# The last attention layer: output projection spread over the recurrence, key sum as a 129th column

## The chip, the cores and the metric

The kernel runs on one core of a Trainium2 chip. The metric is the device time of one execution in microseconds. The program is a chain of four transformer-like layers, each with an attention half and a feed-forward half; the change is inside one half, the attention of the last layer (layer 3).

## The reference

The stream x is one sequence of T = 1024 tokens with D = 256 features. In layer 3 there are H = 16 heads of 128, and the tokens are taken in segments of 64. For each head a memory matrix `mem` (128 x 128) and a divisor `z` (128) are carried from segment to segment:

```python
def step(carry, seg):
    mem, z = carry
    qq, kk, vv = seg
    sigma_q = jax.nn.elu(qq) + 1.0
    scores = jnp.einsum('bhsk,bhtk->bhst', qq, kk) / scale
    scores = jnp.where(causal_mask, scores, -jnp.inf)
    att_dot = jax.nn.softmax(scores, axis=-1) @ vv
    att_mem = sigma_q @ mem / (sigma_q @ z)
    sigma_k = jax.nn.elu(kk) + 1.0
    delta = vv - sigma_k @ mem / (sigma_k @ z)
    mem_new = mem + jnp.einsum('bhsk,bhsv->bhkv', sigma_k, delta)
    z_new = z + sigma_k.sum(axis=-2, keepdims=True).transpose(0, 1, 3, 2)
    att = beta * att_mem + (1.0 - beta) * att_dot
    out = att.reshape(Bsz, SEG, H * DV) @ Wo
    return ((mem_new, z_new), out)
# mem starts at 0, z at 1/128; q, k, v = h @ Wq, h @ Wk, h @ Wv, and x = x + gate * out
```

`att.reshape` lays the heads end to end: rows 4h to 4h + 3 of a segment come from head h alone, and the j-th block of 128 in row 4h + r is that head's token 16r + j of the segment. So the output projection needs, for each j of 0 to 15, four tokens (r = 0 to 3) of every segment of a head, and a pair of heads fills 2 x 64 rows.

## The kernel before

Everything is float32. Features lie on partitions and tokens along the free axis. `l3_attention` (L1917) works through the 16 heads in 8 pairs (numbered 0 to 7 here; `a` is the head in the pair, 0 or 1). Each engine has its own queue, written out by hand as a function `pair(i, ...)`: TensorE from L2024, ScalarE from L2191, VectorE from L2298. The engines meet through semaphores alone, so a wait holds up everything behind it in its queue. PSUM has eight banks of 512 columns. SyncE loads the next pair's weights once the current pair's projections are done, and GpSimd only prepares constants.

The start of a pair on TensorE, in this order: `projections(0)` (keys and queries of head 0, banks 4 to 7, 24 matmuls of 512 columns, L2036), `project_out(i)` (the output projection of the pair before, 32 matmuls, L2021), `scores(0)` (L2068), `values()` for both heads (L2044), `keys_by_token(0)` (turns the keys, L2055), `projections(1)`, `keys_by_token(1)`, `scores(1)`. ScalarE beside it: `queries_keys` (exp into `e`, L2197, and a copy into `qk`, L2198) for each 512 columns; `place_keys`, `values_copy`, `exponential` of the scores (L2226) and `keys_copy` (even half of the partitions, L2210). VectorE: `sigma` (elu + 1 in two instructions, L2307 and L2314), `key_sums` (L2320, L2325), the softmax (`read_scores` L2345, `largest` L2351, `shift` L2354, `total` L2359 and L2360, `normalize` L2364), the odd halves of `values_copy` (L2334) and `keys_copy` (L2340), and `add_projection` (L2296), which adds the projected result of the pair before to x.

Then comes the recurrence, 15 steps n = 1 to 15 for both heads. A step is `read_memory(n, a)` for both heads on TensorE (L2091: keys and queries of the segment times `mem`; column 128 of `mem` holds the divisor), then a filler, then `write_memory(n, a)` (L2080), which adds the keys times the delta to the memory that stays in banks 4 and 5. Between them lies a round through two engines: VectorE's `delta` (L2370 reciprocal of the divisor, L2373) makes `dr` from the read, and ScalarE's `mem_copy` (L2221) carries the memory from PSUM to `mem` after the write.

`key_sums(a)` makes all 16 divisors of a head ahead of the recurrence: one sum over each segment's keys, then a running sum in four additions.

The fillers now: `turn_probs` (turns the softmax, L2101) at steps 1, 2, 7 and 8; `local_attention` (L2114), in halves, at steps 3 to 6 and 9 to 12; `turn_reads` (L2127, turns what the queries read) at 13 and 14, and the rest of it after step 15. ScalarE copies or scales what a filler made (`probs_copy` L2230, `dot_scale` L2235) and prepares the next pair's weights (`high_part` L2189); VectorE does the second head's softmax, `low_part` and, at the end, `add_reads` (L2380), which mixes both parts into `att`.

A segment's 64 tokens are ordered by j, then by r (the permutation `turn` does that). `att` lives in the buffer of the layer's normalised input in the projection's order: for each j the 4 tokens of all 16 segments of a head lie in one run of 64. So `local_attention` and `turn_reads` put each segment's 64 columns into PSUM as 16 pieces of 4 columns (16 bytes) through `segment_rows`, and `project_out` reads two runs of 64 elements.

## Time and profile before

| | us |
|---|---|
| median of 3 runs | 2037.61 |
| lowest, highest | 2035.45, 2040.75 |
| the profiled execution | 2039.76 |
| its span, first to last instruction | 2038.0 |
| mean granted clock of TensorE, as a share | 0.933 |
| l3_attention's eight pairs, from 1352.8 to about 1908 | 555 |
| starts of the pairs in the span | 1352.8, 1419.1, 1488.3, 1558.4, 1627.7, 1696.9, 1766.9, 1837.1 |

The profile is of one execution. A timeline row gives start, length, engine, line, what is written from what, the shape and a count; in square brackets stand the idle time of the engine before it and who ended it. A float32 matmul shows as two records; a matmul with the hi and lo parts shows as one. Records of matmuls overlap, so a record's length is its latency, and the rate is the distance from start to start. A group row gives busy us and the mean in ns, then the idle time before the group's instructions and who ended it.

### The profile page before, as it was taken

The numbers are of one execution on the slowest core, as the hardware profiler recorded it, in microseconds if no ns is written. First come the engines' busy times: TensorE is split into PE (matmuls) and PEld (weight loads), VectorE is DVE, ScalarE is ACT, GpSimd is POOL, SyncE is SP. The second block draws the span as 40 slices with busy tenths as digits, with TensorE's granted clock in tenths as the row PEclk, the third lists the DMA queues.
The fourth block names the chain that finished last, engine by engine and source line by source line (L and its number), as shares of the span: only waits on it lengthen the run. The fifth ranks groups of instructions, "written<-read, shape, count | busy, mean of one in ns | idle before, by whom it ended". The sixth has DMA issues, their size and how long they took to land. (4 is left out here: it accounts for less than half of the span.)

```text
span 2038.0 us, 27403 instructions
## 1 busy us (share of the span) xinstructions
PE 1781.8 (87%) x9315; PEld 1440.3 (71%) x9315; DVE 1081.2 (53%) x2163; ACT 872.8 (43%) x1690; POOL 243.9 (12%) x236
## 2 busy tenths in 40 slices
PE   5988786987689999999787969969999899999898
PEld 4676645775568888888644858857888788878755
DVE  2266435233545555555656345566665676567466
ACT  3466424333243343333675334354443444344344
POOL 2010002212022222222101212220000000000000
PEclk8999886998789999999898979979999999999989
DMA  2000030110034334332100023210000000000100
GB/s 103 6 14 11 0 132 0 39 31 0 18 101 114 108 110 118 115 108 82 52 0 15 32 57 114 82 58 17 17 16 0 15 15 15 0 15 0 41 0 21
DMA packets 47075, 91.50 MB, mean 45 GB/s; under 512 B 7697, under 2 KB 24081, under 8 KB 46810
## 3 DMA queue, kind: packets, MB, share of 16 engines
q1 hardware_dynamic: 47026, 90.89, 14.9%
q8 instruction: 26, 0.43, 0.1%
q14 instruction: 23, 0.19, 0.0%
HBM read 89.52 MB, written 1.35 MB: 45 GB/s over the span
## 5 line engine op out<-in xcount | busy, mean ns | idle before, releaser
L438 PE MATMUL bank<-l1m_src_hi,l1m_w_hi 128*128 128x512 f32 x384 | 150.2, 391 | 7.4 <-DVE l1m_src_lo L507 7.4
L438 PE MATMUL bank<-l1m_src_lo,l1m_w_hi 128*128 128x512 f32 x384 | 150.0, 391 | 0.0
L438 PE MATMUL bank<-l1m_src_hi,l1m_w_lo 128*128 128x512 f32 x384 | 149.9, 390 | 0.0
L410 POOL TENSOR_TENSOR l1m_w_lo<-l1m_w,l1m_w_hi 128x512 fp32r<-128x512 f32 x96 | 104.8, 1110 | 325.9 <-ACT l1m_w_hi L475 325.9
L514 DVE TENSOR_TENSOR l1m_a<-l1m_s,bank 128x512 f32<-128x512 f32 x96 | 66.0, 687 | 116.3 <-ACT l1m_s L487 116.3
L491 ACT ACTIVATE l1m_a_hi<-l1m_a 128x512 fp32r<-128x512 f32 x96 | 60.7, 633 | 146.5 <-DVE l1m_a L520 146.5
L2091 PE MATMUL bank<-l_mem,l_sg 128*128 128x129 f32 x480 | 95.0, 316 | 30.2 <-ACT l_mem L2221 15.4
L2091 PEld LDWEIGHTS bank<-l_mem,l_sg 128*128 128x128 f32 x480 | 67.9, 195 | 55.8 <-ACT l_mem L2221 44.4
L528 DVE TENSOR_TENSOR l1m_a_lo<-l1m_a,l1m_a_hi 128x512 fp32r<-128x512 f32 x96 | 66.4, 692 | 70.8 <-ACT l1m_a_hi L491 70.8
L2370 DVE RECIPROCAL l_inv<-bank 128x1 f32<-128x1 f32 x240 | 38.9, 162 | 115.4 <-PE bank L2091 115.4
L2221 ACT ACTIVATE l_mem<-bank 128x128 f32<-128x128 f32 x240 | 59.8, 276 | 90.5 <-PE bank L2080 90.0
L2080 PE MATMUL bank<-l_dr,l_nkt 128*128 128x128 f32 x480 | 89.8, 304 | 8.3 <-ACT l_dr L2249 8.0
L487 ACT ACTIVATE l1m_s<-bank 128x512 f32<-128x512 f32 x96 | 57.4, 598 | 87.7 <-PE bank L438 87.7
L438 PEld LDWEIGHTS bank<-l1m_src_hi,l1m_w_hi 128*128 128x128 f32 x384 | 72.5, 189 | 24.1 <-issue 9.1
L2373 DVE SCALAR_TENSOR_TENSOR l_dr<-bank,l_inv,l_v 128x128 f32<-128x128 f32 x240 | 84.2, 351 | 8.5
L438 PEld LDWEIGHTS bank<-l1m_src_lo,l1m_w_hi 128*128 128x128 f32 x384 | 72.5, 189 | 15.1
L438 PEld LDWEIGHTS bank<-l1m_src_hi,l1m_w_lo 128*128 128x128 f32 x384 | 72.5, 189 | 15.0
L2080 PEld LDWEIGHTS bank<-l_dr,l_nkt 128*128 128x128 f32 x480 | 68.4, 196 | 17.1 <-ACT l_dr L2249 7.9
L452 PE MATMUL bank<-l1m_a_hi,l1m_w_hi 128*128 128x512 f32 x192 | 74.8, 390 | 0.8 <-DVE l1m_a_lo L528 0.8
L452 PE MATMUL bank<-l1m_a_lo,l1m_w_hi 128*128 128x512 f32 x192 | 74.7, 389 | 0.0
L452 PE MATMUL bank<-l1m_a_hi,l1m_w_lo 128*128 128x512 f32 x192 | 74.7, 389 | 0.0
L2501 POOL MEMSET l3f_imp<- 96x2048 f32 x1 | 1.8, 1806 | 573.7 <-POOLq L88 573.7
(537 smaller groups left out, 4561.9 us busy)
## 6 DMA issues: line engine op xcount, KB each, us to landing
l1m_w<-in_l1f_win SPq DMA_DIRECT2D x48, 256.0 KB, 2.9
l1m_wr<-l1f_token_weights SPq DMA_DIRECT2D x32, 384.0 KB, 3.5
l1m_wr<-l1f_token_weights SPq DMA_DIRECT2D x32, 256.0 KB, 3.9
l_w<-in_l_w SPq DMA_DIRECT2D x9, 768.0 KB, 4.4
wmod<-in_wmod SPq DMA_DIRECT2D x4, 1536.0 KB, 10.1
l1m_w<-in_l1f_wout SPq DMA_DIRECT2D x48, 128.0 KB, 3.1
l1m_wr<-l1f_token_weights SPq DMA_DIRECT2D x32, 128.0 KB, 3.2
l2e_wr<-l2f_token_weights SPq DMA_DIRECT2D x16, 256.0 KB, 3.9
```

Source lines behind the costliest of these rows:

```text
L410: pool.tensor_tensor(w_lo[:, half, part], w[:, half, part], w_hi[:, half, part].bitcast(F32), ALU.subtract).then_inc(split_, 1)
L438: last = pe.matmul(k.bank[:, 2 * c + part, :], wq[:, half, at:at + P], xq[:, b, chunk(c)], start=(b == 0 and q == 0), stop=(b == DB - 1 an ...
L452: last = pe.matmul(k.bank[:, 4 + 2 * m + c, :], wq[:, half, at:at + P], aq[:, c, :], start=(first and q == 0 and not extra), stop=False, s ...
L487: act.activation(s[:, c, :], k.bank[:, 2 * c, :], ACT.Silu).then_inc(act_ready, 1)
L491: act.activation(a_hi[:, c, :], a[:, c, :], ACT.Identity).then_inc(hi_ready, 1)
L514: last = dve.tensor_tensor(a[:, c, :], s[:, c, :], k.bank[:, 2 * c + 1, :], ALU.mult)
L528: dve.tensor_tensor(a_lo[:, c, :], a[:, c, :], a_hi[:, c, :].bitcast(F32), ALU.subtract).then_inc(lo_ready, 1)
L2080: pe.matmul(k.bank[:, MEM + a, 0:P], nkt[:, a, n // 2, n % 2, :], dr[:, a, n, :], start=(n == 0), stop=False, skip_group_check=True).then_ ...
L2091: pe.matmul(k.bank[:, READ + a, 0:P + 1], sg[:, a, n // 2, at:at + 2, :], mem[:, a, n, 0:P + 1], start=True, stop=True).then_inc(s["read_r ...
L2221: act.activation(mem[:, a, n + 1, 0:P], k.bank[:, MEM + a, 0:P], ACT.Identity).then_inc(s["mem_copied"], 1)
L2370: dve.reciprocal(inv[:, a, n % 2:n % 2 + 1], k.bank[:, READ + a, P:P + 1]).then_inc(s["inv_ready"], 1)
L2373: dve.scalar_tensor_tensor(dr[:, a, n, :], k.bank[:, READ + a, 0:P], inv[:, a, n % 2:n % 2 + 1], v[:, n // 2, a, n % 2, :], ALU.mult, ALU. ...
```

## The change

- `project_out` leaves the start of a pair. It is cut in 7 parts (`Y_AT`) of 5, 5, 5, 5, 4, 4 and 4 matmuls, the fillers of steps 1 to 7; `add_projection` moves to step 8. The result bank is 3 instead of 4, and `local_attention(0, 1)` waits for `x_added`.
- The other fillers move back: `turn_probs` for both halves at steps 8 and 10, `local_attention`, now whole, at 9, 11, 12 and 13, `turn_reads` at 14 and 15. ScalarE's `probs_copy`, `dot_scale` and `high_part` and VectorE's `low_part` move with them. All four `add_reads` come after step 15.
- `key_sums` is gone, and the wait for `z_ready` with it. `dr` has a 129th column of -1, and `write_memory` multiplies the negated keys by 129 columns, so the key sum builds up in column 128 of the bank; `first_divisor` puts 1/128 there, and `mem_copy` copies 129 columns. `mem` has 2 slots instead of 16.
- `att` keeps each segment's 64 columns together. `local_attention` and `turn_reads` write 64 columns in one run, and `project_out` reads, for each j, 32 pieces of 4 elements (16 bytes) through `att_by_row`.
- In the start `values()` goes ahead of `scores(0)` and waits for `reads_added`. ScalarE does both `values_copy` ahead of `exponential(0)`, both halves of `keys_copy(0)`, and `place_keys(1)` last. VectorE does both `values_copy` ahead of `read_scores(0)`, and `sigma(4)` and `sigma(5)` ahead of `total(0)`. The banks of values and scores are exchanged.

```diff
+    MEM, READ, Y, SCORES = 4, 6, 3, (5, 0)
+    V_BANKS = (0, 2)
+    Y_AT = (0, 5, 10, 15, 20, 24, 28, 32)
...
+        first_z = sb("first_z", [P, P + 2])
+        mem = sb("mem", [P, HP, 2, P + 2])
+        dr = sb("dr", [P, HP, NS, P + 2])
...
-            return rows_of(bank)[:, :, n * R:(n + 1) * R]
+        att = k.h
+        att_by_row = k.h[:].rearrange("p a (g j r) -> p (a g) j r", j=H, r=R)
...
-                step.link(pool, pool.memset(z[:], 0.0))
-                step.link(pool, pool.memset(z[:, 0, :, PAD:PAD + 1], 1.0 / P))
+                step.link(pool, pool.memset(first_z[:], 0.0))
+                step.link(pool, pool.memset(first_z[:, P:W1], 1.0 / (P * P)))
+                step.link(pool, pool.memset(dr[:, :, :, P:P + 2], -1.0))
...
-                def project_out(turn):
-
-                    pe.wait_ge(s["att_ready"], turn * HP)
-                    for m in range(DB):
-                        for j in range(H):
-                            last = pe.matmul(k.bank[:, Y, m * P:(m + 1) * P], wo[:, j, tile(m)], att[:, :, j, :],
-                                             start=(j == 0), stop=(j == H - 1))
-                    last.then_inc(s["y_ready"], 1)
+                def project_out(turn, part):
+
+                    if part == 0:
+                        pe.wait_ge(s["reads_added"], turn * 4)
+                    for mj in range(Y_AT[part], Y_AT[part + 1]):
+                        m, j = mj // H, mj % H
+                        last = pe.matmul(k.bank[:, Y, m * P:(m + 1) * P], wo[:, j, tile(m)], att_by_row[:, :, j, :],
+                                         start=(j == 0), stop=(j == H - 1))
+                    if part == len(Y_AT) - 2:
+                        last.then_inc(s["y_ready"], 1)
...
-                                if n == Y - MEM and not first:
-                                    pe.wait_ge(s["x_added"], i)
...
                         for t in range(TT):
                             at = V_BANKS[t // 4] + t // 2 % 2
+                            if not first and t == 0:
+                                pe.wait_ge(s["reads_added"], i * 4 - 2)
+                            if not first and t == 4:
+                                pe.wait_ge(s["reads_added"], i * 4)
...
+                    def first_divisor(a):
+
+                        pe.matmul(k.bank[:, MEM + a, 0:W1], k.ones[:], first_z[:, 0:W1], start=True, stop=False,
+                                  skip_group_check=True)
...
-                        pe.matmul(k.bank[:, MEM + a, 0:P], nkt[:, a, n // 2, n % 2, :], dr[:, a, n, :], start=(n == 0),
+                        pe.matmul(k.bank[:, MEM + a, 0:W1], nkt[:, a, n // 2, n % 2, :], dr[:, a, n, 0:W1], start=False,
                                   stop=False, skip_group_check=True).then_inc(s["mem_ready"], 1)
...
-                        pe.matmul(k.bank[:, READ + a, 0:P + 1], sg[:, a, n // 2, at:at + 2, :], mem[:, a, n, 0:P + 1],
+                        pe.matmul(k.bank[:, READ + a, 0:W1], sg[:, a, n // 2, at:at + 2, :], mem[:, a, n % 2, 0:W1],
...
                         if c == 0:
                             pe.wait_ge(s["probs_ready"], i * HP + (a + 1))
+                            pe.wait_ge(s["scores_read"], i * HP + 2)
...
-                    def local_attention(a, c, part):
-
-                        if part == 0:
-                            pe.wait_ge(s["pt_copied"], i * 4 + (2 * a + c + 1))
-                            if a:
-                                pe.wait_ge(s["dot_scaled"], i * 4 + (c + 1))
-                            else:
-                                pe.wait_ge(s["scores_read"], i * HP + 2)
-                        for t in range(4 * c + 2 * part, 4 * c + 2 * part + 2):
+                    def local_attention(a, c):
+
+                        pe.wait_ge(s["pt_copied"], i * 4 + (2 * a + c + 1))
+                        if a:
+                            pe.wait_ge(s["dot_scaled"], i * 4 + (c + 1))
+                        elif 2 + c == Y and not first:
+                            pe.wait_ge(s["x_added"], i)
+                        for t in range(4 * c, 4 * c + 4):
                             for o in range(2):
-                                last = pe.matmul(segment_rows(2 + c, 2 * (t % 4) + o), v[:, t, a, o, :],
+                                at = (t % 4) * P + o * S
+                                last = pe.matmul(k.bank[:, 2 + c, at:at + S], v[:, t, a, o, :],
                                                  pt[:, a, t, o * S:(o + 1) * S], start=True, stop=True)
-                        if part:
-                            last.then_inc(s["dot_ready"], 1)
+                        last.then_inc(s["dot_ready"], 1)
...
-                            half = HALF[1 - n % 2]
-                            last = pe.matmul(segment_rows(2 * a + c, n % 8), dr[:, a, n, :], turn[:, half], start=True,
-                                             stop=True)
+                            at = (n % 8) * S
+                            last = pe.matmul(k.bank[:, 2 * c + a, at:at + S], dr[:, a, n, 0:P], turn[:, HALF[1 - n % 2]],
+                                             start=True, stop=True)
...
                     pe.wait_ge(s["w_split"], i * DB + DB)
                     projections(0)
-                    if not first:
-                        pe.wait_ge(s["qk_copied"], i * 8 + 1)
-                        project_out(i)
+                    values()
                     scores(0)
-                    values()
                     keys_by_token(0)
                     projections(1)
                     keys_by_token(1)
                     scores(1)
                     for a in range(HP):
+                        first_divisor(a)
+                    for a in range(HP):
                         write_memory(0, a)
                     for n in range(1, NS):
                         for a in range(HP):
                             read_memory(n, a)
-                        if n in (1, 2):
-                            turn_probs(0, n - 1)
-                        if 3 <= n <= 6:
-                            local_attention(0, (n - 3) // 2, (n - 3) % 2)
-                        if n in (7, 8):
-                            turn_probs(1, n - 7)
-                        if 9 <= n <= 12:
-                            local_attention(1, (n - 9) // 2, (n - 9) % 2)
-                        if n in (13, 14):
-                            turn_reads(n - 13, 0, range(0, 8))
+                        if n <= 7 and not first:
+                            project_out(i, n - 1)
+                        if n in (8, 10):
+                            for c in range(NCH):
+                                turn_probs((n - 8) // 2, c)
+                        if n in (9, 11):
+                            local_attention(0, (n - 9) // 2)
+                        if n in (12, 13):
+                            local_attention(1, n - 12)
+                        if n in (14, 15):
+                            turn_reads(n - 14, 0, range(0, 8))
                         if n < NS - 1:
                             for a in range(HP):
                                 write_memory(n, a)
...
-                project_out(PAIRS)
+                for part in range(len(Y_AT) - 1):
+                    project_out(PAIRS, part)
...
@@ -2209,6 +2218,10 @@
+                        if a == 0:
+                            act.activation(nkt[ODD, a, :, 1, :], k.bank[ODD, at:at + 2, :].rearrange(
+                                "p n (t q) -> p (n t) q", q=P), ACT.Identity, scale=-1.0
+                                ).then_inc(s["kt_odd_copied"], 1)
...
-                        act.activation(mem[:, a, n + 1, 0:P], k.bank[:, MEM + a, 0:P], ACT.Identity
+                        act.activation(mem[:, a, (n + 1) % 2, 0:W1], k.bank[:, MEM + a, 0:W1], ACT.Identity
                                        ).then_inc(s["mem_copied"], 1)
...
                     for j in range(4):
                         queries_keys(j)
                     place_keys(0)
                     values_copy(0)
+                    values_copy(1)
                     exponential(0)
-                    values_copy(1)
                     keys_copy(0)
                     for j in range(4, 8):
                         queries_keys(j)
+                    keys_copy(1)
+                    act.activation(dr[:, :, 0, 0:P], v[:, 0, :, 0, :], ACT.Identity, scale=-1.0
+                                   ).then_inc(s["first_ready"], 1)
                     place_keys(1)
-                    keys_copy(1)
-                    act.activation(dr[:, :, 0, :], v[:, 0, :, 0, :], ACT.Identity, scale=-1.0
-                                   ).then_inc(s["first_ready"], 1)
                     for n in range(NS - 1):
                         for a in range(HP):
                             mem_copy(n, a)
-                        if n in (0, 1):
-                            probs_copy(0, n)
                         if n == 2:
                             exponential(1)
-                        if n in (3, 5):
-                            dot_scale(0, (n - 3) // 2)
-                        if n in (6, 7):
-                            probs_copy(1, n - 6)
-                        if n in (8, 10) and not final:
-                            high_part(i + 1, (n - 8) // 2)
+                        if n in (3, 5) and not final:
+                            high_part(i + 1, (n - 3) // 2)
+                        if n in (8, 10):
+                            for c in range(NCH):
+                                probs_copy((n - 8) // 2, c)
                         if n in (9, 11):
-                            dot_scale(1, (n - 9) // 2)
+                            dot_scale(0, (n - 9) // 2)
+                        if n in (12, 13):
+                            dot_scale(1, n - 12)
...
-                    def key_sums(a):
-
-                        dve.wait_ge(s["sigma_ready"], i * 8 + (4 * a + 2))
-                        step.link(dve, dve.tensor_reduce(
...
                     for j in range(4):
                         sigma(j)
-                    key_sums(0)
                     if not first:
-                        dve.wait_ge(s["att_ready"], i * HP)
+                        dve.wait_ge(s["reads_added"], i * 4)
                     step.link(dve, dve.tensor_copy(bt[:, 0, :], beta[:, bass.ds(i * HP, HP)]))
                     step.link(dve, dve.tensor_scalar(bt[:, 1, :], bt[:, 0, :], -1.0, 1.0, ALU.mult, ALU.add))
-                    if not first:
-                        add_projection(i)
+                    values_copy(0)
+                    values_copy(1)
                     read_scores(0)
                     largest(0)
                     shift(0)
-                    values_copy(0)
+                    for j in range(4, 6):
+                        sigma(j)
                     total(0)
                     normalize(0, 0)
                     normalize(0, 1).then_inc(s["probs_ready"], 1)
-                    values_copy(1)
-                    keys_copy(0)
-                    for j in range(4, 8):
+                    for j in range(6, 8):
                         sigma(j)
                     keys_copy(1)
-                    key_sums(1)
                     read_scores(1)
...
-                        if n in (10, 12) and not final:
-                            low_part(i + 1, (n - 10) // 2)
-                        if n == NS - 2:
-                            dve.wait_ge(s["dot_scaled"], i * 4 + 4)
-                            add_reads(0, 0)
-                    add_reads(1, 0)
-                    for a in range(HP):
-                        add_reads(a, 1).then_inc(s["att_ready"], 1)
+                        if n in (7, 9) and not final:
+                            low_part(i + 1, (n - 7) // 2)
+                        if n == 8 and not first:
+                            add_projection(i)
+                    dve.wait_ge(s["dot_scaled"], i * 4 + 4)
+                    for c in range(NCH):
+                        for a in range(HP):
+                            add_reads(a, c)
```

## Rows read from the trace of the kernel before

In the rows of busy time by stretch stand the stretch, its length, then busy us and records of TensorE, its weight loads, VectorE, ScalarE and GpSimd, then the granted clock, the DMA share and GB/s.

**Rows 1.** The profile page, part 1: busy time of each engine.

```profile
PE 1781.8 (87%) x9315; PEld 1440.3 (71%) x9315; DVE 1081.2 (53%) x2163; ACT 872.8 (43%) x1690; POOL 243.9 (12%) x236
```

**Rows 2.** Busy time by stretch: pair 4 (start, steps 1-7, steps 8-15).

```profile
1627.70:1658.10 30.40, 28.96 (x247) 26.20 (x246) 23.34 (x41) 15.60 (x26) 0.00 (x0) 1.00 0.09 26
1658.10:1675.00 16.90, 14.70 (x101) 12.24 (x101) 11.42 (x40) 6.66 (x20) 0.00 (x0) 1.00 0.00 0
1675.00:1696.90 21.90, 20.36 (x162) 18.71 (x161) 10.61 (x37) 6.84 (x20) 0.00 (x0) 1.00 0.00 0
```

**Rows 3.** Timeline of TensorE, pair 4, up to the second read.

```profile
1633.22 7.30 PE L2021 MATMUL bank<-h_modulated,l_wo 128*128 128x128 f32 x64
1640.45 1.15 PE L2068 MATMUL bank<-l_qk 128*64 128x64 f32 x32
...
1647.38 1.04 PE L2055 MATMUL bank<-ident,l_keys 128*128 128x128 f32 x8
...
1657.23 0.71 PE L2080 MATMUL bank<-l_dr,l_nkt 128*128 128x128 f32 x4 [0.99 <-ACT l_dr L2249]
...
1659.43 0.48 PE L2091 MATMUL bank<-l_mem,l_sg 128*128 128x129 f32 x2 [0.85 <-DVE l_mem L2325]
```

**Rows 4.** Timeline of TensorE, pair 4, inside the recurrence.

```profile
1663.53 0.71 PE L2091 MATMUL bank<-l_mem,l_sg 128*128 128x129 f32 x4 [0.16 <-ACT l_mem L2221]
1664.08 1.00 PE L2114 MATMUL bank<-l_qk,l_v 128*128 128x64 f32 x8
...
1665.73 0.75 PE L2091 MATMUL bank<-l_mem,l_sg 128*128 128x129 f32 x4
...
1668.26 0.71 PE L2091 MATMUL bank<-l_mem,l_sg 128*128 128x129 f32 x4 [0.45 <-ACT l_mem L2221]
...
1672.98 0.71 PE L2091 MATMUL bank<-l_mem,l_sg 128*128 128x129 f32 x4 [0.45 <-ACT l_mem L2221]
...
1674.99 0.93 PE L2091 MATMUL bank<-l_mem,l_sg 128*128 128x129 f32 x4
...
1689.75 0.71 PE L2091 MATMUL bank<-l_mem,l_sg 128*128 128x129 f32 x4
1690.30 1.90 PE L2127 MATMUL bank<-l_turn,l_dr 128*128 128x64 f32 x16
...
1692.84 0.71 PE L2091 MATMUL bank<-l_mem,l_sg 128*128 128x129 f32 x4
1693.39 3.68 PE L2127 MATMUL bank<-l_turn,l_dr 128*128 128x64 f32 x32
```

**Rows 5.** Groups of instructions on VectorE over pair 4.

```profile
L2307 DVE TENSOR_SCALAR l_e<-l_e 128x512 f32<-128x512 f32 x8 | 3.4, 426 | 1.4 <-ACT l_e L2197 0.9
...
L2364 DVE TENSOR_TENSOR ln_square<-l_sc,l_st 64x512 f32<-64x512 f32 x4 | 2.7, 684 | 0.1
...
L2340 DVE TENSOR_SCALAR l_nkt<-bank 64x1024 f32<-64x1024 f32 x2 | 2.5, 1226 | 0.0
L2320 DVE TENSOR_REDUCE l_z<-l_keys 128x16 f32<-128x1024 f32 x2 | 2.4, 1216 | 0.0
```

**Rows 6.** Groups of instructions on ScalarE over pair 4.

```profile
L2197 ACT ACTIVATE l_e<-bank 128x512 f32<-128x512 f32 x8 | 4.8, 598 | 7.5 <-PE bank L2036 7.5
...
L2210 ACT ACTIVATE l_nkt<-bank 64x1024 f32<-64x1024 f32 x2 | 2.0, 1007 | 0.0
```

**Rows 7.** Busy time by stretch: around the first reads (pairs 5, 4).

```profile
1725.40:1728.80 3.40, 1.41 (x9) 0.99 (x8) 3.20 (x7) 1.49 (x4) 0.00 (x0) 1.00 0.44 176
1728.80:1732.20 3.40, 3.40 (x15) 3.10 (x16) 2.08 (x8) 1.04 (x3) 0.00 (x0) 0.50 0.00 0
1657.10:1660.50 3.40, 2.19 (x13) 1.57 (x13) 3.14 (x10) 0.69 (x4) 0.00 (x0) 1.00 0.23 90
```

**Rows 8.** Busy time by stretch: pair 0, up to its first read.

```profile
1352.80:1379.30 26.50, 23.85 (x180) 20.22 (x180) 20.85 (x35) 15.68 (x26) 0.00 (x0) 0.93 0.11 30
```

**Rows 9.** Busy time by stretch: the matmuls of L1421 (64 columns, another layer).

```profile
539.30:541.00 1.70, 1.70 (x16) 1.70 (x16) 0.00 (x0) 0.83 (x1) 0.00 (x0) 0.99 0.00 0
```

More of the change, by code:

```diff
@@ L1920, in l3_attention @@
     nc, d = k.nc, k.dram
-    H, HP, S, PAD = 16, 2, 64, 8
+    H, HP, S = 16, 2, 64
     PAIRS, NS = H // HP, T // S
     R = S // H
+    W1 = P + 1
     CHAIN = HP * (NS - 1)
@@ L2315, in sigma @@
                                                  ALU.add, ALU.max).then_inc(s["sigma_ready"], 1)
-                    def key_sums(a):
-                        dve.wait_ge(s["sigma_ready"], i * 8 + (4 * a + 2))
-                        step.link(dve, dve.tensor_reduce(
-                            z[:, 0, a, PAD + 1:], keys[:, a].rearrange("p (g q) -> p g q", q=S), AX.X, ALU.add))
-                        for n in range(4):
-                            src, by = z[:, n % 2, a], 1 << n
-                            dst = mem[:, a, :, P] if n == 3 else z[:, (n + 1) % 2, a, PAD:PAD + NS]
-                            ins = dve.tensor_tensor(dst, src[:, PAD:PAD + NS], src[:, PAD - by:PAD + NS - by], ALU.add)
-                            if n < 3:
-                                step.link(dve, ins)
-                            else:
-                                ins.then_inc(s["z_ready"], 1)
                     def values_copy(c):
@@ L2372, in delta @@
                         dve.wait_ge(s["inv_ready"], at)
[L2373 removed]
+                        dve.scalar_tensor_tensor(dr[:, a, n, 0:P], k.bank[:, READ + a, 0:P],
                                                  inv[:, a, n % 2:n % 2 + 1], v[:, n // 2, a, n % 2, :], ALU.mult,
@@ L2431, in _ @@
                 with dve.Fori(1, PAIRS - 1) as i:
-                    step.enter(i - 1, 16)
+                    step.enter(i - 1, 8)
                     pair(i, False, False)
```

31 lines of the change are left out of this document (11 added, 20 removed).

## The prediction

> **What bounds the kernel now.** I read the page first, then the busy time of one pair of heads cut in three, then TensorE's timeline of that pair, then the groups on VectorE and ScalarE. TensorE is busy 87% of the run, VectorE 53% and ScalarE 42% [rows 1]. The change is inside l3_attention, eight pairs of heads, each some 69 us. Pair 4, from its first projection at 1627.66 to the next pair's at 1696.9, is the clean one: granted clock 1.00 throughout [rows 2]. It falls into a start of 30.4 us up to the first read_memory, steps 1 to 7 of the recurrence in 16.9 us, and steps 8 to 15 with the last turns in 21.9 us. In the start TensorE hardly pauses: only 0.99 us ahead of the first write and 0.85 us between the first two reads, and this second wait is for key_sums on VectorE [rows 3]. The reader should see that project_out (7.3 us) sits in this start, while VectorE has nothing to do beside it.
>
> In the recurrence one step has a fixed part and a filler. A step with 8 filler records takes 1665.73 - 1663.53 = 2.20 us, one with 16 takes 1692.84 - 1689.75 = 3.09 us [rows 4]. So a filler record costs 0.11 us and the fixed part is about 1.35 us (each float32 matmul shows as two records). With only 4 records the step still takes 1674.99 - 1672.98 = 2.01 us: there the round through ScalarE's memory copy and VectorE's delta is the limit. Some steps are 0.33 us longer, those whose read waited 0.45 us for the memory copy [rows 4]: ScalarE had dot_scale in hand.
>
> **The start of a pair, after.** project_out leaves it: 64 records, 7.2 us [rows 3]. Is what remains set by TensorE? If so the first read comes at 30.4 - 7.2 = 23.2 us. I followed the new order of the three queues instead, in us from the pair's start. TensorE: projections 5.5, values another 5.8, scores(0) 1.15 [rows 3]; scores(0) now comes behind values, so it ends at 12.5. VectorE is in values_copy(1) until 12.8, then read_scores, largest and shift at 0.69 each, as all of its instructions of that size [rows 5]: 14.9. ScalarE waits for that in exponential(0), 0.6 us [rows 6]: 15.5. Behind this wait in ScalarE's queue stand keys_copy(0), now both halves, 2 x 1.01 less 0.1 of overlap [rows 6], to 17.4, and the second head's queries_keys: exp to 18.0. TensorE finished that projection at about 15, so here it no longer matters. VectorE idles from 14.9 to 18.0, then does sigma(4) and sigma(5), each 0.43 + 0.69, the first with 0.1 of waiting for the copy [rows 5]: 20.4. total and the two normalizes, 0.68 + 0.20 + 2 x 0.69: 22.7. sigma(6), sigma(7): 24.9. keys_copy(1), 1.23 [rows 5]: 26.1. The second head's first write_memory waits for this. With 0.3 us for the write the first read starts at 26.4; the second read has to wait for the copy of the second head's memory, until 27.0, which counts as a start of 26.75. Bounds: 23.2 if none of these waits bites, 27.8 if ScalarE also loses a microsecond on the way. A third view is in between: pair 0 of before has no project_out and took 26.5 us at clock 0.93 [rows 8], some 1.8 us of it lost to the low clock at its beginning, so 24.7. I take 26.75, as the chain is worked out from the new order, and pair 0 ran the old one. So 7.2 us leave and only 3.65 are gained. key_sums, 1.22 and some 0.8 us for each head [rows 5], costs nothing at the first head (VectorE idled there) and at the second shortens step 1.
>
> **The recurrence, after.** Fillers in records: 10, 10, 10, 10, 8, 8, 8 (project_out), 8 (turns of both halves of the probabilities), 16, 8, 16, 16, 16 (local_attention and one turn of probabilities), 16, 16 (turn_reads), then 32 as now. At 1.36 + 0.113 per record of project_out, steps 1 to 4 take 2.49 and 5 to 7 take 2.26: 16.75 us, against 16.9 [rows 2]. Step 8: 2.2. Step 9: 3.05 and 0.2 for local_attention, which waits for the probabilities' copy behind the memory copies on ScalarE. Step 10: 2.2. Steps 11 to 13: 3.05 each, step 14: 3.09. From the last read to the pair's end 1696.9 - 1692.84 = 4.05 with 32 records [rows 4], 5.8 with 48. Sum 25.75 us, against 21.9 [rows 2]: 3.85 more. The delays by dot_scale should vanish, since it is now ready when ScalarE comes to it; that is in the sum. low_part and add_projection (0.95 and 0.9 us) fit in VectorE's 1.4 us between two pairs of deltas: nothing. The memory copy, write and dr operand with a 129th column: nothing, as reads with 129 columns step like writes with 128. first_divisor, 4 records of 0.11, lies in the wait for keys_copy(1). All four add_reads now follow the last delta. The first two are still done before the turns end, the last two end 1.4 us into the next pair, as now; values, which waits for them, starts at 5.5. POOL's memsets, the DMAs' triggers and the end (project_out after the last pair, 7.2 us, bare as now) are unchanged.
>
> For a clean pair: 26.75 + 16.75 + 25.75 = 69.25, against 69.2. What leaves the start comes back in steps 9 to 15.
>
> **The 16-byte pieces.** project_out's moving operand becomes 32 pieces of 4 elements. Today it reads pieces of 64 and takes 0.113 us a record [rows 3]; no row shows such reads from SBUF. Below: no gain, as full-width records with 64 or 128 columns take 0.11 alike [rows 3, 4]. Above: double, 64 x 0.11 = 7 us a pair. I take nothing. The outputs of local_attention and turn_reads in PSUM go the other way, from 16-byte pieces to one run. The nearest rows say nothing is gained: in pieces 0.11 us a record [rows 4], and the matmuls of L1421, which write 64 columns in one run, 16 in 1.70 us, 0.106 each [rows 9]. The Trainium skill, in "SBUF — State Buffer", section "Door 1: The DMA port swizzle", says that SBUF lines are 16 bytes and at least two hits to a line keep full rate, and that a PSUM pattern which isn't contiguous slows matmuls much. The first half agrees with my price of nothing, which no row here tests; the second speaks for a gain that these rows don't show.
>
> **The clock.** In pair 5 TensorE was busy 1.41 of 3.40 us ahead of and around the first read, and the next stretch was granted 0.50, the 1.2 GHz level; in pair 4 it was busy 2.19 and kept 1.00 [rows 7]. Pair 5 is 0.8 us longer for it. Pairs 0, 2, 5, 6 and 7 fell so, once each. After, TensorE is out of work from about 23 to 26 us in nearly every pair: turn of keys, scores(1), the divisors, then nothing until keys_copy(1). I expect a fall in nearly every pair, and a dearer one: the steps behind it are now filled to 95% (10 records of 0.11 and 8 more in 2.49 us) and stretch to some 4.05 us at half clock, so 3.4 us cost 1.3. Against 0.8 in four of seven pairs now, that is +0.8 us a pair; bounds -0.45 (no falls) and +2.2 (two stretches).
>
> **Pair 0** has nothing to fill steps 1 to 7. Start 26.75 + 1.8 = 28.6, against 26.5 [rows 8]: +2.1. Seven steps at 2.0 us [rows 4], up to 2.45 at the low clock, some 16 us instead of 16.9 [rows 2] and 0.8 for its fall: -1.7. Later steps: +3.85. Sum +4.
>
> **The sum.** Pairs 1 to 7: 7 x (0.05 + 0.8) = +6; pair 0: +4. The profiled execution took 2039.76 us (span 2038.0), so 2050 for it; it stands 2.15 above the median of 2037.61, so 2048.
>
> **Rivals.** (1) The start is bound by TensorE after all: ScalarE and VectorE keep up, first read at 23.2, no more clock falls than now. Per pair 23.2 + 16.75 + 25.75 = 65.7, so -3.5 x 7 plus about 2 for pair 0: 2015. For it: VectorE idles 3.1 us beside project_out today. Against it: the chain above, and pair 0, where VectorE never paused without project_out. It needs exponential(0) not to block ScalarE. (2) The clock isn't hurt more than now: 7 x 0.05 + 4, 2042, within the bound of no change. Pair 4's example speaks for it, the 3 us hole against it. (3) Reading in 16-byte pieces costs double: 7 steps of 1.1 us more each, 7 x 7 = +49, about 2095. It decides from the first step: project_out's records at 0.2 us at full clock. Nothing in the trace shows it. (4) Contiguous outputs free TensorE: local_attention and turn_reads at half, 128 x 0.055 = 7 us a pair, 8 pairs: 1992. This is the skill's PSUM rule at work; rows 9 speak against it.
>
> **Chances.** Forecast (2044 to 2060) 0.52, rival 1 0.15, rival 2 0.22, rival 3 0.06, rival 4 0.05. A measurement here tells some 0.3% (6.1 us) from no change: slower 0.58, same 0.22, faster 0.20. The likeliest case alone spans 2044 to 2060. To leave out no more than 0.2 I go down to 2026, half way to rival 1, since the start may land between 23.2 and 26.75: 2026 to 2060.
>
> **What would show it.** First read of a clean pair at 26 to 27 us from its start with VectorE's keys_copy(1) as releaser; ScalarE idle some 2 us ahead of exponential(0); steps 1 to 4 at 2.5 us, 9 to 15 at 3.05; project_out's records at 0.11; a stretch at 0.50 near the first read of most pairs; no wait of 0.45 for the memory copy. If the first read comes by 24 us, the start was mis-sized and the kernel is faster; if project_out's steps exceed 3 us at full clock, rival 3 holds.

## The result

The changed kernel takes 2051.94 us (median; 2050.28 to 2054.03), the kernel before 2039.18 beside it (2035.45 to 2043.88). The ratio is 1.0064, 95% interval 1.0046 to 1.0081: slower, by 12.8 us or 0.6%. 2048 had been forecast, with a range of 2026 to 2060. The profiled execution took 2052.14 us, span 2050.4, granted clock 0.928.

Part 1 of the page after, which answers to [rows 1]: TensorE has 32 records more (first_divisor), VectorE 88 instructions less (80 of the key sums, and 8 copies of keys_copy(0) that ScalarE now does).

```profile
PE 1785.6 (87%) x9347; PEld 1447.8 (71%) x9347; DVE 1044.2 (51%) x2075; ACT 882.1 (43%) x1698; POOL 244.2 (12%) x237
```

That says nothing of 12 us. What does is the distance from one pair's first projection to the next, taken from TensorE's timeline:

| us | pair 0 | 1 | 2 | 3 | 4 | 5 | 6 |
|---|---|---|---|---|---|---|---|
| before | 66.24 | 69.24 | 70.14 | 69.21 | 69.23 | 70.05 | 70.15 |
| after | 75.22 | 70.67 | 69.29 | 70.67 | 69.29 | 70.67 | 69.30 |

Of the 12.4 us by which the span grew, pair 0 has 9.0, pairs 1 to 6 have 1.9, pair 7 and what follows 0.8, and what lies ahead of the pairs 0.7. A fall of the clock is a stretch in which TensorE is granted half of it; the clean pair, one without a fall, is as long as it was.

Busy time by stretch, after, pair 2, cut as in [rows 2]: start, steps 1 to 7, the rest.

```profile
1499.40:1526.00 26.60, 22.39 (x186) 19.45 (x186) 18.67 (x31) 16.46 (x26) 0.00 (x0) 1.00 0.11 30
1526.00:1542.70 16.70, 15.62 (x123) 14.09 (x122) 11.04 (x36) 5.67 (x18) 0.00 (x0) 1.00 0.00 0
1542.70:1568.70 26.00, 25.06 (x205) 23.53 (x205) 10.78 (x41) 8.03 (x23) 0.00 (x0) 1.00 0.00 0
```

The start is 3.8 us shorter though 7.2 us of TensorE's work have left it: TensorE is idle 4.2 of 26.6 us there (before 1.4 of 30.4). The last stretch is 96% busy and 4.1 us longer.

TensorE's timeline ahead of the first read of that pair, and its first filler:

```profile
1519.95 1.09 PE L2057 MATMUL bank<-ident,l_keys 128*128 128x128 f32 x8 [1.51 <-DVE l_keys L2326]
1521.13 1.15 PE L2070 MATMUL bank<-l_qk 128*64 128x64 f32 x32
1522.21 0.71 PE L2076 MATMUL bank<-l_first_z,ones 128*128 128x129 f32 x4
1522.76 0.39 PE L2087 MATMUL bank<-l_dr,l_nkt 128*128 128x129 f32 x2
1525.76 0.46 PE L2087 MATMUL bank<-l_dr,l_nkt 128*128 128x129 f32 x2 [2.61 <-issue]
1526.05 1.02 PE L2097 MATMUL bank<-l_mem,l_sg 128*128 128x129 f32 x4
1526.91 1.28 PE L2020 MATMUL bank<-h_modulated,l_wo 128*128 128x128 f32 x10
1528.03 0.61 PE L2087 MATMUL bank<-l_dr,l_nkt 128*128 128x129 f32 x4
```

Two waits: 1.51 us for sigma(5)'s keys, and 2.61 us between the two heads' first writes, called the hole below. The profile calls the second one "issue"; what it waited for is seen on VectorE, where keys_copy(1), the last of these rows of its timeline, ends at 1525.66, 0.1 us ahead of the write:

```profile
1513.61 0.69 DVE L2352 TENSOR_TENSOR l_sc<-l_sc,l_st 128x512 f32<-128x512 f32 x1
1517.58 0.43 DVE L2319 TENSOR_SCALAR l_e<-l_e 128x512 f32<-128x512 f32 x1 [3.28 <-ACT l_e L2206]
...
1519.81 0.68 DVE L2357 TENSOR_REDUCE l_st<-l_sc 128x8 f32<-128x512 f32 x1
1520.53 0.20 DVE L2358 RECIPROCAL l_st<-l_st 128x8 f32<-128x8 f32 x1
1520.76 1.38 DVE L2362 TENSOR_TENSOR ln_square<-l_sc,l_st 64x512 f32<-64x512 f32 x2
...
1524.43 1.23 DVE L2338 TENSOR_SCALAR l_nkt<-bank 64x1024 f32<-64x1024 f32 x1
```

VectorE idles 3.28 us with the softmax's input at hand from ScalarE at 1514.96, then does 2.3 us of total and normalize between sigma(5) and sigma(6), when TensorE waits for what comes behind them.

The clock, which answers to [rows 7], and pair 0 [rows 8]: busy time by stretch around the hole of pair 1, the same stretches of pair 2, and pair 0's start and what follows.

```profile
1451.70:1455.10 3.40, 0.78 (x7) 0.62 (x7) 3.27 (x6) 1.13 (x3) 0.00 (x0) 1.00 0.02 5
1456.70:1460.10 3.40, 3.40 (x17) 3.16 (x17) 1.00 (x3) 0.56 (x2) 0.00 (x0) 0.53 0.00 0
...
1522.40:1525.80 3.40, 0.79 (x7) 0.63 (x6) 3.27 (x6) 1.11 (x3) 0.00 (x0) 1.00 0.05 21
1527.40:1530.80 3.40, 3.25 (x30) 3.06 (x28) 2.28 (x7) 0.50 (x2) 0.00 (x0) 1.00 0.00 0
...
1353.50:1381.90 28.40, 24.20 (x183) 20.75 (x184) 17.22 (x29) 16.46 (x26) 0.00 (x0) 0.92 0.09 28
1381.90:1400.00 18.10, 17.27 (x55) 13.18 (x56) 10.47 (x35) 5.61 (x16) 0.00 (x0) 0.50 0.00 1
```

Pairs 1 and 2 have the same hole, and behind it pair 1 gets 3.4 us at the 1.2 GHz level (from 1.1 us after its first read) and is 1.38 us longer, while pair 2 keeps 2.4 GHz. So it goes on: 1, 3, 5 and 7 fall, 2, 4 and 6 don't. In pair 0 the fall lasts 23.9 us.

### The profile page after: what moved, and what is told of

Read it like the earlier page. It is cut to its first block and busy times, and to the rows that moved or that the text cites. A ratio compares the mean times of both kernels' runs of the same rounds, so it can differ in the third digit from the quotient of the medians.

```text
span 2050.4 us, 27324 instructions
## 1 busy us (share of the span) xinstructions
PE 1785.6 (87%) x9347; PEld 1447.8 (71%) x9347; DVE 1044.2 (51%) x2075; ACT 882.1 (43%) x1698; POOL 244.2 (12%) x237
## 3 DMA queue, kind: packets, MB, share of 16 engines
HBM read 89.52 MB, written 1.35 MB: 44 GB/s over the span
## 5 line engine op out<-in xcount | busy, mean ns | idle before, releaser
L2234 ACT ACTIVATE l_mem<-bank 128x129 f32<-128x129 f32 x240 | 62.3, 279 | 217.1 <-PE bank L2087 216.3
L2087 PE MATMUL bank<-l_dr,l_nkt 128*128 128x129 f32 x480 | 86.5, 302 | 21.7 <-issue 20.9
L2020 PE MATMUL bank<-h_modulated,l_wo 128*128 128x128 f32 x512 | 70.4, 289 | 1.3 <-DVE h_modulated L2378 1.3
```

The costliest lines, as they stand in the source:

```text
L2020: last = pe.matmul(k.bank[:, Y, m * P:(m + 1) * P], wo[:, j, tile(m)], att_by_row[:, :, j, :], start=(j == 0), stop=(j == H - 1))
L2087: pe.matmul(k.bank[:, MEM + a, 0:W1], nkt[:, a, n // 2, n % 2, :], dr[:, a, n, 0:W1], start=False, stop=False, skip_group_check=True).then ...
L2234: act.activation(mem[:, a, (n + 1) % 2, 0:W1], k.bank[:, MEM + a, 0:W1], ACT.Identity).then_inc(s["mem_copied"], 1)
```

## The experiments

The theory by then: the length of a clean pair is made of three things that nearly cancel: the fill gains, work moved to steps 9 to 15 costs, and the new order of the start costs; the hole that this order leaves on TensorE takes the clock down. The rivals: the fill itself or the 16-byte pieces hold no gain; pair 0 loses the clock because its steps are empty and not because of the hole.

**1. Pair 0 gets filler.** The changed kernel with matmuls whose result nobody reads, where the later pairs have project_out:

```diff
                         if n <= 7 and not first:
                             project_out(i, n - 1)
+                        if n <= 7 and first:
+                            for mj in range(Y_AT[n - 1], Y_AT[n]):
+                                pe.matmul(k.bank[:, Y, 2 * P:3 * P], ...)
```

> The changed kernel, with steps 1 to 7 of pair 0 filled too: the same 32 matmuls of project_out, on whatever the buffer holds, into unused columns of bank 3. Theory (the 24 us at half clock in pair 0 come from steps with 8 records and nothing else): the clock returns after one stretch, steps 1 to 7 at 2.42 and 2.2 us once it has, pair 0 falls from 75.2 to about 71 us, the rest is unchanged: 4 us less, about 2048. Rival (the low clock of pair 0 has another cause, such as its start after a long pause): it stays low, the steps stretch to some 4 us each, pair 0 takes 84 us or more, about 2061.

Measured: 2045.93 us, ratio 1.0027 (1.0015 to 1.0038). The half clock in pair 0 shrank from 23.9 to 6.8 us, yet pair 0 went only from 75.22 to 74.22: its first two steps took 4.37 and 3.15 us (low clock and filler together), the next 2.42. The rest of the gain is no effect of the filler on pair 0: the falls now lie in pairs 2, 4 and 6, one fewer; the pairs begin 2.2 us earlier, and from pair 7 on the run is another 2.3 us shorter, beyond the fall that pair 7 is spared; nothing was changed there. About 71 had been expected for pair 0, so that miss is 3 us. The filler holds the clock up but costs what it gives back.

**2. Softmax ahead of sigma(4).** The changed kernel, VectorE's order alone:

```diff
                     shift(0)
-                    for j in range(4, 6):
-                        sigma(j)
                     total(0)
                     normalize(0, 0)
                     normalize(0, 1).then_inc(s["probs_ready"], 1)
-                    for j in range(6, 8):
+                    for j in range(4, 8):
                         sigma(j)
```

> The changed kernel, with total(0) and both normalize(0) ahead of sigma(4) and sigma(5) on VectorE. Theory (the start is bound by the chain exponential(0), keys_copy(0), queries_keys(4) on ScalarE and then sigma, softmax, sigma, keys_copy(1) on VectorE, with VectorE idle 3.3 us in its middle): the softmax's 2.3 us move into the idle time, first read 24.4 us after the pair's start instead of 26.7, a clean pair 67.0 instead of 69.3, eight pairs 18 us less: about 2034. Rival (TensorE or ScalarE binds the start): first read within 0.3 us of 26.7, time within 3 us of the changed kernel's.

Measured: 2023.49 us, ratio 0.9917 (0.9900 to 0.9934). First read at 24.30 us into the pair instead of 26.66, every pair 66.9, and no fall of the clock in any pair, pair 0 (66.77) among them. TensorE's wait of 1.51 us stays and the one of 2.61 is gone, as its timeline shows:

```profile
1510.03 1.09 PE L2057 MATMUL bank<-ident,l_keys 128*128 128x128 f32 x8 [1.51 <-DVE l_keys L2326]
...
1513.46 0.46 PE L2087 MATMUL bank<-l_dr,l_nkt 128*128 128x129 f32 x2 [0.24 <-issue]
1513.75 1.02 PE L2097 MATMUL bank<-l_mem,l_sg 128*128 128x129 f32 x4
```

Three calls moved ahead of two others, into an idle stretch, are worth 28 us: in the two profiled executions some 19 in eight pairs at 2.37 or more and some 11 of clock, less the 2 us by which this run's pairs begin later.

**3. The hole filled.** The changed kernel with ten matmuls between the first two writes, whose result nobody reads:

```diff
-                    for a in range(HP):
-                        write_memory(0, a)
+                    write_memory(0, 0)
+                    for t in range(10):
+                        pe.matmul(k.bank[:, READ, P + 128:P + 256], k.ident[:], k.ones[:], start=True, stop=True)
+                    write_memory(0, 1)
```

> The changed kernel, with 10 matmuls of 128 columns (2.2 us, result unused, bank 6) between the first head's first write and the second's, where TensorE stands idle 2.6 us. Theory (the hole makes the clock fall in every second pair): no stretch at half clock in pairs 1 to 7, each 69.3 us, 4 x 1.4 = 5.5 us less, about 2046. Pair 0 keeps its low clock in steps 1 to 7, or loses it later. Rival (the falls don't come from the hole): still four falls, pairs at 70.7 as now, about 2052.

Measured: 2040.72 us, ratio 1.0006 (0.9991 to 1.0021), 11 less than the changed kernel. All of pairs 1 to 6 take 69.28 or 69.29 us: no fall is left in them. Busy time by stretch, the hole of pair 1 in this kernel and the stretch behind it:

```profile
1443.10:1446.50 3.40, 3.02 (x27) 2.85 (x27) 3.27 (x6) 1.05 (x2) 0.00 (x0) 1.00 0.00 0
1446.50:1449.90 3.40, 3.13 (x24) 2.75 (x25) 2.15 (x6) 0.78 (x3) 0.00 (x0) 1.00 0.00 0
```

Apart from the ten matmuls the pair's work is the same and its critical path too, only the hole is gone. So in pairs 1 to 7 the hole is what takes the clock, at 1.38 us a fall. More was gained than expected since pair 0 also got shorter: 72.16, with 10.2 us at half clock instead of 23.9. The profiled execution gives 14.4 us, but 5.6 of these lie ahead of pair 0, where nothing was changed. The ten executions run from 2034 to 2046 us at mean granted clocks from 0.940 to 0.933, and one of them was profiled (2037.69), so that no fall is left is shown for that one.

Pair 0, whose steps 1 to 7 are empty, falls here without a hole, in step 5:

```profile
1382.60:1386.00 3.40, 2.57 (x13) 1.61 (x12) 2.46 (x10) 1.54 (x4) 0.00 (x0) 0.99 0.00 0
1386.00:1396.20 10.20, 9.83 (x37) 8.38 (x38) 5.29 (x16) 2.73 (x9) 0.00 (x0) 0.50 0.00 1
```

TensorE was busy 2.57 of the 3.40 us ahead of this fall, and this same kernel's pairs 1 to 7 keep the clock though TensorE still waits 1.51 us in each of them. So a hole isn't the only thing that can take the clock, and the busy share just ahead doesn't settle it.

**4. The projection back at the start, new order kept.**

```diff
                     projections(0)
+                    if not first:
+                        for part in range(len(Y_AT) - 1):
+                            project_out(i, part)
                     values()
                     scores(0)
...
-                        if n <= 7 and not first:
-                            project_out(i, n - 1)
```

> The changed kernel, with project_out back behind projections(0) in the start of a pair (bank 4, add_projection ahead of values_copy(1), as before) and steps 1 to 7 without a filler; key column, contiguous outputs and the other fillers stay. Theory (filling is worth 7.2 us of work less what the bare steps save, and bare steps lose the clock): first read at 33.9 us, steps 1 to 7 at 2.6 us under a low clock as in pair 0, later steps as now plus 1 us, a pair about 80 us, some 2125 in all. Rival (the clock holds without fillers): steps at 2.0 us, a pair 74.2, about 2086. Third (the later start hides project_out, as the start's chain isn't on TensorE): a pair at 70 or less, at most 2057.

Measured: 2118.49 us (one run), pairs of 79.3 to 80.4. After the hole the empty steps run at half clock, 2.61 us each. Busy time by stretch, pair 1:

```profile
1463.00:1466.30 3.30, 0.95 (x6) 0.79 (x6) 3.05 (x6) 0.28 (x1) 0.00 (x0) 1.00 0.00 0
1466.30:1486.80 20.50, 20.50 (x68) 15.77 (x68) 12.13 (x38) 5.89 (x17) 0.00 (x0) 0.50 0.01 1
```

So filler decides how long a fall lasts: 3.4 us in filled steps (6.8 in pair 0 of run 1), 20.5 to 23.9 in empty ones, where it ends in step 8 or 9, as the fillers begin.

**5. The old order of the start.** The changed kernel with TensorE's scores(0) ahead of values, ScalarE's exponential(0) between the two values_copy and half of keys_copy(0), and VectorE's order as before without the key sums:

```diff
                     projections(0)
-                    values()
                     scores(0)
+                    values()
...
-                    values_copy(0)
-                    values_copy(1)
                     read_scores(0)
                     largest(0)
                     shift(0)
-                    for j in range(4, 6):
-                        sigma(j)
+                    values_copy(0)
                     total(0)
                     normalize(0, 0)
                     normalize(0, 1).then_inc(s["probs_ready"], 1)
-                    for j in range(6, 8):
+                    values_copy(1)
+                    keys_copy(0)
+                    for j in range(4, 8):
                         sigma(j)
```

> The changed kernel, with the start of a pair in the order that the kernel before has on all three engines, only without project_out and key_sums: scores(0) ahead of values on TensorE, exponential(0) between the two values_copy on ScalarE, the odd half of keys_copy(0) back on VectorE, values_copy, softmax, keys_copy(0) and then four sigma on VectorE. Theory (the new order, not the recurrence, ate half of what project_out left): first read at 23 us instead of 26.7, a clean pair 65.7, eight pairs some 29 us less, about 2023, so faster than before. Rival (the old order has its own waits once nothing lies between projections(0) and scores(0)): first read at 25 or later, at least 2038.

Measured: 2018.42 us, ratio 0.9895 (0.9878 to 0.9912). First read at 23.95, pair 66.58, steps 1 to 7 and the rest to 0.01 us as in the changed kernel, no fall. Against run 2 (66.93) the rest of the old order, that of TensorE and ScalarE and of VectorE's copies, is worth 0.35 us.

**6. The key sum as a column, alone.** The kernel before without key_sums, with first_divisor and the 129th column:

```diff
-                        pe.matmul(k.bank[:, MEM + a, 0:P], nkt[...], dr[:, a, n, :], start=(n == 0),
+                        pe.matmul(k.bank[:, MEM + a, 0:P + 1], nkt[...], dr[:, a, n, 0:P + 1], start=False,
...
-                    key_sums(0)
...
-                    key_sums(1)
```

> The kernel before, with only its key sums replaced by the column of -1 in dr, the first divisor in the bank and 129 columns in the memory's copy. Theory: step 1 loses its wait of 0.85 us for key_sums and VectorE's delay of the first delta, 0.7 us a pair, up to 1.5 where the first delta waited longest; the first head's key_sums lay in idle time. Eight pairs: 6 to 12 us less, about 2030, and fewer falls of the clock. Rival (another wait ends as late: the second half of keys_copy on VectorE): within 3 us of before.

Measured: 2019.4 us, ratio 0.9898 (0.9878 to 0.9919). Clean pairs of 68.05 us against 69.23, and no fall in any pair. The wait of 0.85 us in [rows 3] and what followed it were key_sums(1): the first interval of the recurrence went from 3.20 to 2.01 us, all others stayed. With reads at an even pace from the start the falls of the kernel before, 0.8 to 0.9 us each, are gone too; that the pace is the reason is argued, as no run changes it alone. 6 to 12 us had been expected, 19 were found.

**7 and 8. What else the start holds.** In run 5 TensorE still waits before scores(0):

```profile
1497.21 1.15 PE L2070 MATMUL bank<-l_qk 128*64 128x64 f32 x32 [1.18 <-ACT l_qk L2207]
```

Run 7 is run 5 with half of the values there, and ScalarE doing both halves of keys_copy(0); run 8 has the values in halves only.

```diff
                     projections(0)
+                    values(0)
                     scores(0)
-                    values()
+                    values(1)
```

> The changed kernel with the start in the order of the kernel before on VectorE and ScalarE, but on TensorE the first half of the values ahead of scores(0) and the second half behind it, and both halves of keys_copy(0) on ScalarE. In the old order TensorE waits 1.17 us between projections(0) and scores(0) (5.73 to 6.90 us into a pair) and its first read is at 23.95; from 14.64 on it hardly waits. If TensorE's own work bounds the start there, the half of the values fills that wait and the first read comes at about 22.8 to 23.0, the pair at 65.5 instead of 66.58, the kernel at about 2010. If VectorE's chain bounds it (values_copy(1) behind the softmax, then sigma(4) to sigma(7), then keys_copy(1)), the first read stays near 23.9 and the time at 2018.

> As the run with the values in halves, but VectorE keeps its half of keys_copy(0) (1.22 us ahead of sigma(4)). If VectorE's chain is the second bound of the start, right behind TensorE, nearly nothing comes of the 1.17 us: keys_copy(1) still ends at about 23.5, first read 23.6 to 23.9, pair 66.3 to 66.6, kernel 2015 to 2018. If the start is TensorE's alone, this run gives the same 65.5 and 2010 as the one with ScalarE's keys_copy.

Measured: 2006.16 us, ratio 0.9838 (0.9816 to 0.9860), first read at 22.70, pair 65.33; and for the halves alone 2012.88, ratio 0.9867 (0.9841 to 0.9894), first read at 23.51, pair 66.15. With halves alone a new wait stands ahead of keys_by_token(1), for sigma(5), which VectorE reaches late; with ScalarE's keys_copy it is gone. TensorE's timeline, first of the halves alone, then of run 7:

```profile
1502.54 1.09 PE L2057 MATMUL bank<-ident,l_keys 128*128 128x128 f32 x8 [0.67 <-DVE l_keys L2323]
```

```profile
1501.88 1.04 PE L2057 MATMUL bank<-ident,l_keys 128*128 128x128 f32 x8
1503.21 1.15 PE L2070 MATMUL bank<-l_qk 128*64 128x64 f32 x32 [0.30 <-ACT l_qk L2208]
```

The order that the expectations looked for holds: TensorE bounds the start first, VectorE right behind. The first came out a little better than priced (22.70, 65.33 and 2006 for 22.8 to 23.0, 65.5 and 2010); of the second, 23.51 and 66.15 lie just under the stated 23.6 to 23.9 and 66.3 to 66.6, and 2012.88 between the two branches, so the halves alone give a little more than nearly nothing. Run 7 is 45.8 us faster than the changed kernel, 33 faster than the one before.

**9. What the filling is worth.** Run 5 with the whole of project_out ahead of scores(0) and steps 1 to 7 empty (the edit of run 4).

> The changed kernel with the old order of the start and the whole output projection back between projections(0) and scores(0), steps 1 to 7 of the recurrence without filler: what the filling alone is worth. If a fall of the clock needs an idle stretch of TensorE just ahead of the recurrence (the changed kernel has one of 2.4 us, the old order has none), the empty steps run at the full clock at 2.0 us: first read at 30.4 instead of 23.95 (+6.5), seven steps at 2.0 instead of 2.0 to 2.7 (-2.2), pair 70.9, kernel 18.4 + 7 x 4.3 = 2049. If the thin load of the empty steps alone lowers the clock, the steps take 2.6 us as in the run with the projection at the start of the changed kernel, the pair is about 76 and the kernel about 2084.

Measured: 2040.96 us, ratio 1.0001 (0.9987 to 1.0014), pairs of 70.07. First read at 29.85, empty steps at 1.99 us. Busy time by stretch, pair 2 (start, steps 1 to 7):

```profile
1490.00:1519.80 29.80, 29.41 (x250) 26.73 (x249) 20.78 (x36) 15.49 (x25) 0.00 (x0) 1.00 0.08 20
1519.80:1534.00 14.20, 12.79 (x59) 8.51 (x58) 11.25 (x36) 5.89 (x18) 0.00 (x0) 1.00 0.03 13
```

The same empty steps that ran at half clock in run 4 keep the full clock here in all pairs, where no hole stands ahead of them: a thin load alone need not take it, though pair 0 of run 3 shows that it can. I had expected 2049; the first read came 0.6 earlier than that of the kernel before.

**The whole account, clean pairs in us:**

| kernel | first read at | pair | change |
|---|---|---|---|
| before | 30.43 | 69.23 | |
| + key sum as a column (run 6) | 30.43 | 68.05 | -1.18 |
| + pieces, local_attention and turns late (run 9) | 29.85 | 70.07 | +2.02 |
| + project_out as filler (run 5) | 23.95 | 66.58 | -3.49 |
| + new order of the start (changed kernel) | 26.66 | 69.29 | +2.71 |

Run 9's +2.02 is 16 records of turn_reads more in the tail (5.83 instead of 4.04 us) and steps of 16 records, less 0.6 at the start.

## Why the prediction was right, point by point

**The start: right.** First read expected at 26.4, found at 26.66; with the second read's wait, which stays as a longer first step, 26.75 expected and 26.97 found. The chain went as worked out: the wait of exponential(0) was 2.42 us on ScalarE, VectorE idled 3.28 us (3.1 expected), sigma(6) and sigma(7) stood behind the softmax, and keys_copy(1) began at 1524.43 - 1499.39 = 25.04 (24.9 expected). Runs 2 and 5 show it as the cause: with the softmax moved, 24.30; with the old order, 23.95. Rival 1's 23.2 was the start by TensorE's work alone; run 7 gets there, even to 22.70, and the changed kernel doesn't. Not seen was that the weight within this chain lay so unevenly: the softmax's place alone makes 2.37 of the 2.71 us.

**The recurrence: right.** Steps 1 to 4 take 2.42 us (2.49 expected), 5 to 7 2.2 (2.26), except the first, which has that wait and takes 2.73. The 0.06 too much is a slip in the fixed part of a step: the rows give 2.20 - 8 x 0.11 = 1.32 us, and 1.35 and 1.36 were used. From the pair's start to step 8 that is 43.28 us (43.5); from there on 26.01 (25.75), of which step 9 has 3.38 (3.25); the forecast's own terms add up to 25.69. Steps 12 to 14 take 3.09 (3.05, 3.05 and 3.09) and the tail 5.83 (5.8). The clean pair: 69.29, expected 69.25.

**The 16-byte pieces: right.** Ten records of project_out in 1528.03 - 1526.91 = 1.12 us, 0.112 each as before [rows 3]. Rival 3 falls. local_attention's 16 records with PSUM output in one run: 1547.45 - 1545.62 = 1.83 us,

```profile
1545.62 2.00 PE L2121 MATMUL bank<-l_qk,l_v 128*128 128x64 f32 x16
1547.45 0.66 PE L2087 MATMUL bank<-l_dr,l_nkt 128*128 128x129 f32 x4
```

0.114 each with the small wait inside. A step with 16 records of turn_reads takes 3.09 us in both kernels, in pieces before [rows 4] and in one run after. Rival 4 falls, since half had to show. Of the two rules in the Trainium skill's "SBUF — State Buffer", section "Door 1: The DMA port swizzle", the one for SBUF, that two hits to a 16-byte line keep full rate, agrees with these rows (0.112 for 16-byte pieces); the one for PSUM, that a pattern which isn't contiguous slows matmuls, is not seen with outputs of 64 columns in pieces of 16 bytes.

**The clock: its price right, its count wrong.** A fall costs 1.38 us (1.3 expected). But it comes in four pairs of the seven, as before, and not in nearly every one: in this point rival 2 was right. Pairs 1 to 6 gave +1.9 where about +5 was expected. The step that failed took a hole with a low busy share as sufficient for a fall; the rows of pairs 1 and 2 above, 0.78 and 0.79 us busy of 3.40 and one fall, refute that. The trace of the kernel before held the same answer: [rows 7] set 1.41 us busy in pair 5, which fell, against 2.19 in pair 4, which didn't, but the stretches lie at different places, 28.5 and 29.4 us into their pairs. At the same place pair 4 shows 1.41 too:

```profile
1656.20:1659.60 3.40, 1.41 (x9) 0.99 (x8) 3.20 (x7) 1.48 (x4) 0.00 (x0) 1.00 0.49 197
1725.40:1728.80 3.40, 1.41 (x9) 0.99 (x8) 3.20 (x7) 1.49 (x4) 0.00 (x0) 1.00 0.44 176
```

So what TensorE did just ahead told the falling pairs from the others neither before nor after. Run 3 shows that without the hole pairs 1 to 7 have none.

**Pair 0: mis-sized.** +4 expected, +9.0 found. The start was right, 28.77 (28.6). But steps 1 to 7 took 18.70 us instead of 16, and the rest 27.75 instead of 25.75: the fall went on for 23.9 us, through all seven steps and into step 9. The forecast had put a step at the low clock at 2.45 us at most and only some of the seven there; they take 2.61. Run 2, whose pair 0 keeps the clock with the same empty steps, takes 66.77. So of the 9.0 us only 0.5 is moved work (against a pair 0 of before with a short fall of its own), 2.6 is the order of the start (first read at 26.15 there) and 5.8 is clock. The two errors, 5 us too little here and some 3 to 4 too much in the later pairs, partly cancel: 2048 against 2051.9 owes something to that.

**Key sums: under-priced.** "Shortens step 1" was priced at nothing of its own; alone it gives 1.18 us a pair and ends the falls, 19 us in all (run 6), of which the traces show 11.7 in pairs 0 to 6 and 5.3 behind (2.1 of them in pair 7's start and recurrence, the rest unexplained). In the changed kernel, by the account above, the moved fillers and the new start take it back.

## What to carry to other kernels

Filling idle steps frees time only if the path that work leaves is then short on the other engines too: write out each queue anew, and put what is ready early (here a softmax) into an idle stretch instead of between two things that TensorE waits for. A hole of 2.6 us on TensorE costs more than itself, for the clock behind it may fall, for 3.4 us in dense steps (1.38 us lost) and for over 20 in thin ones. Where a change bundles several edits, time each against the others: here two good ones (-1.18, -3.49) were hidden by a bad one (+2.71) and a neutral-looking one (+2.02).

## What the runs showed of the hardware

A steady thin recurrence (12.79 us of TensorE's work in 14.2 us, run 9) keeps 2.4 GHz; the same after 3.3 us with 0.95 busy runs 20.5 us at 1.2 GHz (run 4). Neither is a rule: pair 0 of run 3 fell for 10.2 us in thin steps with no hole ahead, 2.57 us busy of 3.40, and pair 4 of the kernel before kept its clock behind 1.41 of 3.40. One and the same hole brings a fall in every second pair, about 139.9 us apart (from 1456.5, 1596.4, 1736.4 and 1876.3); why the others are spared stays open. The first pair begins between 1347.9 and 1357.4 us in the eleven traces of this case, each of another kernel, though the work ahead of it is the same in all, so small differences between two kernels are better read from the pairs than from the total.
